# Two graph-attention layers on one core: where in a group of four steps the second table's write is issued

## The reference, cut to what matters

```python
h = relu(layernorm(x))                       # x: 8192 x 128, f32
hw = h @ W                                   # layer 0
e = leaky_relu((hw @ a1)[:, None] + (hw @ a2)[None, :], 0.2)
x = x + elu(softmax(where(adj > 0, e, NEG), axis=1) @ hw)

h = relu(layernorm(x))                       # layer 1
q, k, v = h @ Wq.T + bq, h @ Wk.T + bk, h @ Wv.T + bv
s = q @ k.T / sqrt(128)
x = x + elu(softmax(where(adj > 0, s, NEG), axis=-1) @ v)
```

## Time and profile before

| | |
|---|---|
| runs shown | 1710.78 us median of 3 (1709.91 to 1712.45) |
| profiled execution | 1709.7 us, span of its instructions 1708.0 us |
| first phase, from the trace | about 0 to 956 us; the adjacency loads end before 863 us |
| second phase | about 957 to 1708 us |
| busy over the span | PE 68%, DVE 72%, ACT 51%, POOL 67% |
| DMA | 372.42 MB; q1 (SP) 289.83 MB, q0 (POOL's gathers) 81.08 MB |

### The profile page before, as it was taken

One profiled execution on the slowest core, in us unless ns is written; L12 is line 12 of the kernel. 1 busy time (PEld: TensorE's weight loads), 2 busy tenths in 40 slices (PEclk: granted clock), 3 DMA queues, 4 the chain that ended last, 5 costly groups with the idle time before them and its releaser, 6 DMA issues.

```text
span 1708.0 us, 23183 instructions
## 1 busy us (share of the span) xinstructions
PE 1161.2 (68%) x5314; PEld 919.1 (54%) x5362; DVE 1235.4 (72%) x6788; ACT 875.2 (51%) x1763; POOL 1137.7 (67%) x1206
## 2 busy tenths in 40 slices
PE   2667775776777777667765567766766677677765
PEld 1344553554544454455444467655666666666664
DVE  3567996998888898888897366656665665665665
ACT  2768876777777778777752222333233233322322
POOL 1237775766666766667667477777777777777773
PEclk9878877777777777777765555666666666666655
DMA  9879999999999999999932122222222222222221
GB/s 294 344 256 386 395 395 399 396 397 374 371 389 382 390 381 381 387 377 381 392 82 62 48 59 58 65 64 65 64 66 65 65 64 64 65 65 63 65 65 41
DMA packets 122264, 372.42 MB, mean 218 GB/s; under 512 B 34577, under 2 KB 67858, under 8 KB 89362
## 3 DMA queue, kind: packets, MB, share of 16 engines
q1 hardware_dynamic: 75458, 289.83, 44.2%
q0 software_dynamic: 38464, 81.08, 17.0%
q10 hardware_dynamic: 8208, 0.03, 0.3%
HBM read 358.12 MB, written 12.72 MB: 217 GB/s over the span
## 4 chain that ended last, share of the span: by engine, by line
POOL 34%; DVE 20%; DMA 15%; issue 13%; PE 10%; ACT 6%; SPq 2%; POOLq 0%; ACTq 0%; DVEq 0%
POOL arena L609 32%; DMA table<-arena 13%; ACT arena L1186 4%; PE psum L1445 4%; PE psum L1431 3%; POOL arena L579 2%; DMA arena<-in_adj_dram 1%; DVE arena L765 1%; DVE arena L798 1%; DVE arena L873 1%; DVE arena L768 1%; DVE arena L880 1%; PE psum L1417 1%; DVE arena L889 1%; SPq L452 1%
## 5 line engine op out<-in xcount | busy, mean ns | idle before, releaser
L579 POOL DMA_INDIRECT arena<-table,arena x576 | 556.1, 966 | 263.8 <-issue 159.6
L609 POOL DMA_INDIRECT arena<-table,arena x576 | 553.2, 960 | 184.1 <-issue 175.0
L1186 ACT ACTIVATE arena<-arena 128x2048 bf16<-128x2048 int32 x256 | 485.0, 1895 | 32.7 <-DMA arena<-in_adj_dram 32.7
L1384 PE MATMUL psum<-arena 128*128 128x512 bf16 x976 | 281.6, 433 | 26.3 <-ACT arena L1186 22.3
L880 DVE SCALAR_TENSOR_TENSOR arena<-arena 128x131 f32<-128x131 f32 (+1 forms) x768 | 268.2, 349 | 15.5
L1431 PE MATMUL psum<-arena 128*128 128x131 f32 (+1 forms) x768 | 201.4, 434 | 104.1 <-ACT arena L1319 102.4
L1417 PE MATMUL psum<-arena 128*128 128x18 f32 x768 | 135.4, 308 | 174.5 <-DVE arena L846 174.5
L1431 PEld LDWEIGHTS psum<-arena 128*128 128x128 f32 x768 | 180.6, 331 | 107.8 <-issue 107.8
L1417 PEld LDWEIGHTS psum<-arena 128*128 128x128 f32 x768 | 129.4, 249 | 191.9 <-DVE arena L846 191.6
L1127 DVE CUSTOM_DVE_ANT_0 arena<-arena,psum 128x129 f32<-128x129 f32 x192 | 45.2, 286 | 229.7 <-DMA arena<-table,arena 229.7
L1424 PE MATMUL psum<-arena 128*128 128x1 f32 x768 | 135.7, 292 | 103.0 <-DVE arena L863 101.9
(11 more groups left out here) (204 smaller groups left out, 1989.9 us busy)
## 6 DMA issues: line engine op xcount, KB each, us to landing
arena<-in_adj_dram SPq DMA_DIRECT2D x256, 1024.0 KB, 15.3
arena<-table,arena POOLq DMA_INDIRECT x1152
table<-arena POOLq DMA_DIRECT2D x32, 132.0 KB, 5.2
arena<-table SPq DMA_DIRECT2D x64, 66.0 KB, 13.3
table<-arena SPq DMA_DIRECT2D x16, 256.0 KB, 15.3
arena<-table SPq DMA_DIRECT2D x64, 64.0 KB, 1.9
out_dram<-arena SPq DMA_DIRECT2D x16, 256.0 KB, 2.4
arena<-in_x_dram SPq DMA_DIRECT2D x4, 0.5 KB, 12.1
```

Of the source, the lines that this page charges most:

```text
L579: pool.indirect_dma_start(Gt[:, v % GROUP, c + 1, :], None, table0, bass.IndirectOffsetOnAxis(idx_now[:, v % GROUP, c:c + 1], 0))\
L609: pool.indirect_dma_start(Gt[:, t % GROUP, c + 1, 0:D], None, table1, bass.IndirectOffsetOnAxis(idx_now[:, t % GROUP, c:c + 1], 0))\
L1186: nc.scalar.activation(mask[:, k, q * QUARTER:(q + 1) * QUARTER], adj_sb[:, k, q, :], ACT.Relu, accum_out=sum_all[:, bass.ds(tile, 1), q:q ...
L1384: nc.tensor.matmul(V[k], shifted[:, s, :], mask[:, k, s * 512:(s + 1) * 512], start=(s == 0), stop=False)
```

## The change

In SP's `load_group` the write of a group to `table1` moves. Before, it is issued in step b = 0 of group g for the stage of group g - 4; now in step b = 2 of group g for the stage of group g - 3. The wait on `stage_done` that guards it has the same meaning (all four tiles of that group are in the buffer). With that SP's last group, which held only the last write, falls away.

```diff
-                    if b == 0 and (not isinstance(g, int) or 0 <= g - 4 < G):
-                        sp.wait_ge(stage_done, (g - 3) * GROUP)
+                    if b == 2 and (not isinstance(g, int) or 0 <= g - 3 < G):
+                        sp.wait_ge(stage_done, (g - 2) * GROUP)
                         sp.dma_start(table1[1:N + 1, :].rearrange("(t p) d -> p t d", p=P)
-                                     [:, bass.ds((g - 4) * GROUP, GROUP), :], stage[:, :, :]).then_inc(table1_in, 16)
+                                     [:, bass.ds((g - 3) * GROUP, GROUP), :], stage[:, :, :]).then_inc(table1_in, 16)
-
-            bodies(sp, load_group, 4, 15, 20)
+
+            bodies(sp, load_group, 4, 15, 19)
```

## The result

| | before | after |
|---|---|---|
| median | 1710.78 us (5 runs, 1708.73 to 1712.45) | 1700.73 us (5 runs, 1700.26 to 1703.91) |
| profiled execution | 1709.7 us, span 1708.0 us | 1700.7 us, span 1699.0 us |

The ratio is 0.9948, 95% interval 0.9937 to 0.996: faster, by 10 us. The forecast of 1679.6 us and its range (1659 to 1691) miss it. It is the time that the rival "The transfers were the limit all along" gave, 1701.

A forecast was written before the change was run, and what follows sets the result against it. The first phase was taken as held by ACT's staging waits, then by data at 397 GB/s. Eleven groups of 49.85 us save 27.1 us, the last wait 4.13: together 31.2 off 1709.7, plus 1.1 for the median, 1679.6 us; range 1659 to 1691.

The forecast's parts named there:

- The transfers were the limit all along: Rival, first phase: 382 GB/s is what the mix sustains, waits return at adjacency reads; at most 9.7 us less, 1701; chance 0.11.
- The wait goes: ACT at staging line L1257: the write lands over 12 us early, so all 12 waits, 51.8 us, go.
- SP's added wait costs nothing: SP's queue, step b = 2: the wait on the staging fits into 1.4 us before the next load; costed at nothing.
- The engines' limit is 48.0 us a group: First phase without staging waits: engines need 48.0 us a group; as a rival, reached at 412 GB/s, 1659.2 us, chance 0.10.
- What is late next is the data: First phase: ACT then waits for adjacency instead, since a group's data need 49.85 us against the engines' 48.0.
- At 397 GB/s that is 49.85 us: First phase: a group's 19.79 MB moved at 397 GB/s sets its length; eleven groups gain 27.1 us.
- that state ... to the end of the adjacency: Full queue, ACT waiting for quarters, 396 to 397 GB/s, expected from step 16 (263.80 us) until the adjacency ends.
- The bounds of the rate, 389 to 412: GB/s in the first phase: from the best group with a wait to where engines limit; 389 gives 1690.8 us.
- The loss sits behind the waits: Transfer rate in the first phase: it falls to 359 GB/s just after a staging wait, then recovers to 398.
- The last group's wait of 4.13 us: Staging wait in the group after step 60: it also goes and no wait for data replaces it.
- Own rows late at L852, the slower rival: Rival: own rows on SP's fuller queue make DVE wait 1.7 us every tile, groups 54.8 us; 1734 us, chance 0.04.
- The 358 GB/s of the Trainium skill: HBM-to-SBUF limit cited against the forecast: groups would need an estimated 55.3 us, nothing won; the trace's 382 to 397 disagrees.

The follow-up runs named there:

- e5_two_stages: The kernel before, write in its old place, but with two stage buffers used in turn: 1703.62 us.
- e8_act_write: The changed kernel, with the write to table1 issued by ACT on its own queue behind the staging, not by SP: 1702.19 us.
- e6_three_gathers: The changed kernel, with three of POOL's nine gathers of a tile kept in the first phase from tile 4 on: 1649.68 us.
- e4_sp_rows: The changed kernel, with POOL's nine gathers of a first-phase tile replaced by one load of fixed rows, same bytes, on SP's queue: 1688.74 us.
- e9_pool_plain: The changed kernel, with POOL's nine indirect gathers of a tile replaced by nine plain loads of fixed rows on POOL's queue: 1694.92 us.

## Why the prediction was wrong, and what of it was right

- *The wait goes*: right. All 12 waits at L1257 went, and the writes of the steady stretch land 22.5 to 24.6 us after their issue, in time. (The 23.4 us of the earlier trace rows, taken as the longest landing, is a median, of one write.)
- *SP's added wait costs nothing*: right as far as the runs show it. e5_two_stages, which adds no such wait, has the same time, and so has e8_act_write, where SP doesn't issue the write.
- *The engines' limit is 48.0 us a group*: right, e6_three_gathers shows it at 47.74. It was never reached with nine gathers.
- *What is late next is the data*: right in name. ACT's waits at L1186 and quarters landing in over 20 us came as described.
- ***"At 397 GB/s that is 49.85 us"*, and "that state ... to the end of the adjacency": this step failed.** 397 GB/s was read from 215 to 373 us, in which the lag grew from 4.4 to some 8 us: it counts what fifteen engines got ahead of the sixteenth. A quarter is there when the sixteenth increment is in, and that came at a pace of 51.74 us a group. Eleven groups at 51.74 in place of 49.85 are 20.8 us, and that is nearly all of the miss of 21.1 us. The bounds of the rate, 389 to 412, both lay too high, since the low one was the best stretch and not the mean over a long steady time, 382. The term that was missing is the growth of the lag, 2.4 us a group.
- *"The loss sits behind the waits"*: the rows were read rightly and understood wrongly. After a wait the aggregate did fall, but winning that back won no time: in eight groups 29.5 us of waits went for nothing. That fifteen engines had less to do there while the sixteenth still had work is the reading that fits, not shown by itself: the DMA share of that window is 1.02, with POOL's packets of 4224 bytes at 299 ns in the mean from 494.5 to 505 us, against 176 from 505 to 543.5.
- *The last group's wait of 4.13 us*: gained in part, 2.1 us in that stretch; the wait there was for the write's sixteenth increment as well (852.76, the fifteenth at 846.57).
- *The rival with the right number* argued that a full DMA showed itself at L1257, and that each wait comes back at the adjacency. That is what happened, and it got 0.11. Its cause was not right: it took 382 GB/s for what this mix sustains, and e8_act_write moved 397 to 399 up to 460 us in groups just as long. That its 1701 us is within 1 us of the measured time is partly luck: of its 9.7 us, 4.1 were for the last wait, which gave 2.1. What told for it was in the trace of before, in a view not taken: eleven of the twelve waits began when fifteen of the write's sixteen increments were in.
- *Own rows late at L852, the slower rival*: didn't occur; they land in 17.4 us, sooner than the 20 us or more that was given as a sign of being right.
- *The 358 GB/s of the Trainium skill* ("DMA: Bandwidth & Descriptors", section "Where 436 GB/s comes from"), set against the trace in the prediction, is not borne out: the lowest window of the change from 215 to 803 us is at 377.

Open: why that one engine is slower with POOL's queue, and why the growth isn't in proportion to the gathers (2.4 us a group with 36, 2.1 with 24, 1.6 with 12 while it grew). The Trainium skill, "DMA: Bandwidth & Descriptors", section "Latency and other measured facts", says that DMA engines 7 and 15 are usually slower than the rest in traces, and gives as a best guess a contention around the descriptor rings of POOL's queue. The runs agree that it comes with the transfers on POOL's queue (e4_sp_rows without them, with one on SP's queue for nine; e9_pool_plain with them) and show one late increment in sixteen, not two; which engine it is, and the cause, no run here shows.

## What to carry to other kernels

A transfer is there when its slowest engine is: before moving a wait on a DMA, look at how far its last increment lies behind the last but one, since a wait that one late engine makes comes back at the next transfer that is waited for. A rate read while that lag grows counts what the fast engines get ahead; take the pace from bytes over many stages in which the lag no longer grows.

## What the runs showed of the hardware that was not expected

- The last of the sixteen increments of a 1 MB load comes 12 to 18 us after the first while POOL's queue carries 24 or 36 transfers a group, and under 4 us after it when they are on SP's queue (e4_sp_rows). Fifteen are in within 5 us in either case (stretches of the table, loads not split).
- Loads of 120 + 8 or 112 + 16 rows in place of 128 cost 80 and 65 us over fifteen quarters (1781.12 and 1766.18 against 1700.73 us), 5.4 and 4.4 us each. Even of the small own rows, splitting the loads in 120 + 8 costs 15 us (1715.37).
- An issue on SP's queue that waits for no semaphore can last 8.6 us (L455 in the change) and 10.0 us (L491 in e4_sp_rows); e8_act_write shows that this doesn't set the pace here.
- The DMA share did not tell who waits: it is 0.98 in a window of e6_three_gathers in which the engines are the limit and no one waits for adjacency, and 0.99 to 1.02 after the change, where ACT waits for adjacency:

```profile
705.00:754.00 49.00, 38.59 (x175) 25.73 (x175) 45.94 (x255) 40.44 (x60) 12.28 (x13) 0.79 0.98 375
```
